# Cross-attention and a routed FFN on one core: score chunks of three banks, one scratch bank, other places for the steps, and a reordered prologue

## The reference, cut to what matters

```python
x = x + xattn(layernorm(x), ctx, ctx, mask, W_q, W_k, W_v, W_o)   # x: 32 x 100 x 128, ctx: 32 x 1444 x 128
x = x + ffn(layernorm(x), gate_w, w1, w2)

def xattn(Q, K, V, ...):          # 16 heads of 8
    q, k, v = Q @ W_q.T, K @ W_k.T, V @ W_v.T
    e = exp(clip(q k^T / sqrt(8), -50, 50))      # 100 x 1444 for each head
    return (e / sum(e)) v @ W_o.T

def ffn(x, ...):                  # 8 experts, hidden 512, the best 2 for each token
    probs = softmax(x @ gate_w); best two, weights normalised
    return sum of weight * (gelu(x @ w1[e]) @ w2[e])
```

## Time and profile before

| | us |
|---|---|
| median of 3 runs | 1036.55 |
| lowest and highest | 1033.01, 1038.11 |
| the profiled execution | 1029.2 |
| its span, first to last instruction | 1027.4 |
| first scores | 29.69 |
| one batch of the loop, mean of eight | 25.68 |

### The profile page before, as it was taken

How to read it: one execution, slowest core, us unless ns; L and a number is a source line. 1 busy time by engine, 2 the same in 40 slices (tenths; PEclk the granted TensorE clock), 3 DMA queues, 4 the chain that set the end, 5 groups by cost and what they waited for, 6 DMA issues and landing times.

```text
span 1027.4 us, 31365 instructions
## 1 busy us (share of the span) xinstructions
PE 953.8 (93%) x9974; PEld 695.5 (68%) x9975; DVE 808.5 (79%) x2140; ACT 716.0 (70%) x941; POOL 340.0 (33%) x422
## 2 busy tenths in 40 slices
PE   3799999999999999999999999999999996599980
PEld 2566666666666666666666666666666773599980
DVE  5477888888888888888888888888888985444433
ACT  2577878787878787878787878787878774244430
POOL 3182322222222222222222222222222234255554
PEclk9699999999999999999999999999999999699995
DMA  6755666666666666666666666666666663122216
GB/s 182 182 150 173 186 189 188 186 188 189 186 188 186 189 187 189 186 189 188 187 186 189 186 189 186 189 186 187 189 188 186 184 229 86 41 66 67 66 43 191
DMA packets 312438, 172.70 MB, mean 168 GB/s; under 512 B 205274, under 2 KB 260518, under 8 KB 312406
## 3 DMA queue, kind: packets, MB, share of 16 engines
q1 hardware_dynamic: 131898, 142.19, 42.4%
q10 hardware_dynamic: 175612, 23.48, 14.5%
q0 software_dynamic: 4896, 6.63, 2.1%
HBM read 36.83 MB, written 22.08 MB: 57 GB/s over the span
## 4 chain that ended last, share of the span: by engine, by line
PE 88%; DMA 2%; ACT 2%; issue 2%; SPq 2%; DVE 1%; POOL 1%; ACTq 1%; POOLq 0%; DVEq 0%
PE scores L816 32%; PE o_sum L828 28%; PE scratch L747 7%; PE scratch L756 7%; PE scores L940 5%; PE scores L951 5%; ACT probs L1058 2%; SPq L604 1%; DMA q_stack<-q_rep 1%; ACTq L979 1%; PE scratch L794 1%; DMA x_all<-in_x_dram 1%; PE scratch L751 0%; DMA q_and_ctx<-expert_outputs 0%; POOL rows L688 0%
## 5 line engine op out<-in xcount | busy, mean ns | idle before, releaser
L1058 ACT ACTIVATE probs<-scores 128x800 f32<-128x800 f32 (+1 forms) x640 | 603.8, 973 | 152.2 <-PE scores L816 139.8
L816 PE MATMUL scores<-q_stack,k_stack 128*128 128x400 f32 x1536 | 412.9, 385 | 15.2 <-DMA q_stack<-q_rep 9.2
L1214 DVE TENSOR_SCALAR probs<-probs 128x800 f32<-128x800 f32 (+1 forms) x640 | 402.4, 661 | 16.9 <-ACT probs L1058 11.8
L816 PEld LDWEIGHTS scores<-q_stack,k_stack 128*128 128x128 f32 x1536 | 250.8, 190 | 140.8 <-ACT probs L1058 84.1
L828 PE MATMUL o_sum<-probs,v_both 128*17 128x200 f32 x6144 | 304.0, 335 | 0.0
L828 PEld LDWEIGHTS o_sum<-probs,v_both 128*17 128x17 f32 x6144 | 158.4, 97 | 109.3 <-issue 39.9
L699 POOL DMA_INDIRECT expert_rows<-rows,row_atu x64 | 71.9, 1124 | 322.0 <-DVE row_atu L1301 290.2
L756 PE MATMUL scratch<-w_turned,ctxT 128*128 128x128 f32 x768 | 101.0, 275 | 0.0
L756 PEld LDWEIGHTS scratch<-w_turned,ctxT 128*128 128x128 f32 x768 | 99.7, 191 | 0.7 <-issue 0.3
L747 PE MATMUL scratch<-ctxT,w_turned 128*128 128x512 f32 x186 | 85.3, 567 | 0.0
L1154 DVE COPY v_both<-scratch 128x512 f32<-128x512 f32 x93 | 63.7, 685 | 20.4 <-PE scratch L756 20.4
(11 more groups left out here) (148 smaller groups left out, 665.7 us busy)
## 6 DMA issues: line engine op xcount, KB each, us to landing
k_stack<-k_hi SPq DMA_DIRECT2D x192, 256.0 KB, 3.5
k_stack<-k_lo SPq DMA_DIRECT2D x192, 256.0 KB, 4.8
expert_rows<-fill SPq DMA_DIRECT2D x32, 406.2 KB
q_and_ctx<-in_ctx_dram ACTq DMA_DIRECT2D x15, 720.0 KB
ctx_nat<-in_ctx_dram ACTq DMA_DIRECT2D x15, 720.0 KB
q_rep<-q_parts SPq DMA_DIRECT2D x126, 50.0 KB
q_stack<-q_rep SPq DMA_DIRECT2D x126, 50.0 KB, 2.6
v_both<-expert_rows SPq DMA_DIRECT2D x57, 65.0 KB, 1.8
```

The source lines that it names most:

```text
L816: last = nc.tensor.matmul(score_banks(c)[:, m, :], k_stack[p][:, g, t * P:(t + 1) * P], q_stack[p][:, :, g, :], start=True, stop=True)
L1058: nc.scalar.activation(probs_of(c), score_banks(c), ACT.Exp, scale=SCALE).then_inc(exp_ready, 1)
L1214: nc.vector.tensor_scalar(chunk, chunk, LOW, HIGH, ALU.max, ALU.min).then_inc(probs_ready, 1)
```

## The change

The prologue: POOL clears the query stacks ahead of the first deviations; TensorE projects the first queries ahead of the first key third; ScalarE issues the last part of x and the context load of batch 2 after the exp of chunk 2 of batch 0, no longer ahead of chunk 0. In the loop ScalarE issues the context load of batch b+3 after the exp of chunk 12 of batch b, no longer that of batch b+2 ahead of chunk 0, and two more batches stand behind its loop. VectorE's third context transpose, no longer the first, waits for the load of the overhanging keys.

Chunks: 16 of three units, in two times three banks. One scratch bank is left, so every step uses the same one. Steps, PV halves, transposes, norms and queries have other iterations, counted in 16 and no longer in 20; the order of the steps is another one, with value 0 first and value 1 ahead of the tokens.

```diff
-    UNITS = [3, 2, 3, 2, 3, 2, 3, 2, 2, 2] * 2
+    UNITS = [3] * 16
+    SCRATCH = 1
-    SB0, SB1 = 3, 2
+    SB0, SB1 = 3, 3
-    HALF_AT = [5] * 3 + [8] * 3 + [9] * 2 + [11] * 2 + [15] * 6 + [21] * 4 + [23] * 4
+    HALF_AT = [4] * 2 + [5] * 2 + [7] * 3 + [10] * 3 + [12] * 4 + [15] * 7 + [17] * 3
-    STEPS = [("key", 0), ("project", 0), ("value", 0), ("key", 1), ("key", 2), ("tokens", 0), ("gate", 0),
-             ("value", 1), ("value", 2), ("rank", 0)]
-    STEP_AT = [7, 9, 12, 14, 14, 15, 16, 17, 19, 19]
+    STEPS = [("value", 0), ("key", 0), ("project", 0), ("key", 1), ("value", 1), ("tokens", 0), ("gate", 0),
+             ("key", 2), ("value", 2), ("rank", 0)]
+    STEP_AT = [2, 4, 5, 7, 8, 10, 11, 12, 13, 15]
-    TURN_AT = [0, 7, 11]
-    WEIGHED = 5
-    SPLIT_AT = 15
+    TURN_AT = [0, 1, 1]
+    WEIGHED = 4
+    SPLIT_AT = 11
+    LOAD_AT = 12
+    LATE_X_AT = 2
-    CONTEXT_AT = [3, 6, 8]
-    NORM_AT = [[5, 9, 15], [1, 4, 8, 11]]
-    QUERY_AT = [[6, 10, 17], [2, 5, 10, 13]]
+    CONTEXT_AT = [1, 5, 9]
+    NORM_AT = [[3, 6, 10], [0, 3, 6, 9]]
+    QUERY_AT = [[5, 8, 12], [2, 5, 8, 11]]
-    MOMENTS_AT = {8: 4, 9: 5, 10: 6, 11: 7}
+    MOMENTS_AT = {6: 4, 7: 5, 8: 6, 9: 7}
...
-            invert_deviations(0)
             for p in range(2):
                 nc.gpsimd.memset(q_stack[p][:].bitcast(F32), 0.0).then_inc(q_stack_cleared, 1)
+            invert_deviations(0)
...
             pe.wait_ge(w_turned_ready, 1)
+            pe.wait_ge(ctxT_ready, 2)
-            first_key(0)
             pe.wait_ge(xT_ready, 1)
             project_q(scores[:, 1, :]).then_inc(q_in_psum, 1)
+            first_key(0)
...
-            act.dma_start(x_all[:, X_PARTS[2], :], x[X_PARTS[2]].rearrange("b q d -> q b d")).then_inc(x_loaded[2], 16)

             def attend(b, p):
-                if not (isinstance(b, int) and b + 2 >= B):
...
-                    load_blocks(b + 2, p)
                 for c in range(CHUNKS):
...
                     nc.scalar.activation(probs_of(c), score_banks(c), ACT.Exp, scale=SCALE).then_inc(exp_ready, 1)
+                    if not later(b) and c == LATE_X_AT:
+                        act.dma_start(x_all[:, X_PARTS[2], :], x[X_PARTS[2]].rearrange("b q d -> q b d")).then_inc(x_loaded[2], 16)
+                        load_blocks(2, 0)
+                    if c == LOAD_AT and not (isinstance(b, int) and b + 3 >= B):
+                        if later(b):
+                            act.wait_ge(ctxT_ready, turns_before(b + 1) + KSTEPS)
+                        else:
+                            act.wait_ge(scratch_filled, scratch_step(0, FIRST_STEPS[0].index(("turn", KSTEPS - 1))) + 1)
+                        load_blocks(b + 3, 1 - p)
...
                 if k == 0:
                     dve.wait_ge(ctx_loaded[1 - p], 16 * (i + 1 + p))
+                if k == KSTEPS - 1:
                     dve.wait_ge(ctx_over_loaded[1 - p], 16 * (OVER * (i + p) + 1))
```

More of the change, by code:

```diff
@@ L142, in xattn_moe @@
     X_PARTS = [slice(0, QB), slice(QB, 4 * QB), slice(4 * QB, B)]
-    MOMENTS_AT = {8: 4, 9: 5, 10: 6, 11: 7}
+    MOMENTS_AT = {6: 4, 7: 5, 8: 6, 9: 7}
     BEFORE = ITS_BASE[1] + len(PLANS[1]) - 2 * len(STEPS)
-    assert len(STEPS) == len(STEP_AT) and len(STEPS) % 2 == 0 and BEFORE >= 0
+    assert len(STEPS) == len(STEP_AT) and len(STEPS) % SCRATCH == 0 and BEFORE >= 0
     assert 1 + len(NORM_AT[0]) + len(NORM_AT[1]) == QSTEPS
@@ L160, in scratch_use @@
         if is_first(b):
-            return (ITS_BASE[b] + n) % 2, (ITS_BASE[b] + n) // 2
+            return (ITS_BASE[b] + n) % SCRATCH, (ITS_BASE[b] + n) // SCRATCH
         use = BEFORE + n
-        return use % 2, len(STEPS) // 2 * b + use // 2
+        return use % SCRATCH, len(STEPS) // SCRATCH * b + use // SCRATCH
     def planned(b, c):
@@ L323, in xattn_moe @@
         o_sum = ps("o_sum", [P, 512])
-        scratch = ps("scratch", [P, 2, 512])
+        scratch = ps("scratch", [P, SCRATCH, 512])
         hidden_in = [scores[:, n, :] for n in range(2)]
@@ L363, in xattn_moe @@
         scratch_filled = sem("scratch_filled")
-        scratch_emptied = [sem(f"scratch_emptied{n}") for n in range(2)]
+        scratch_emptied = [sem(f"scratch_emptied{n}") for n in range(SCRATCH)]
         k_hi_ready = sem("k_hi_ready")
@@ L862, in _ @@
             for step, (name, k) in enumerate(ALONE):
-                into_scratch(name, k, 0, 0, None, (step % 2, step // 2))
+                into_scratch(name, k, 0, 0, None, (step % SCRATCH, step // SCRATCH))
             pe.wait_ge(mask_cast, 1)
@@ L1039, in _ @@
                     nc.scalar.copy(v_ones[0][:, k * KC:(k + 1) * KC, :, 0:2 * DH],
-                                   scratch[:, step % 2, :].rearrange("p (t n d) -> p t n d", t=KC, n=PAIRS)
-                                   ).then_inc(scratch_emptied[step % 2], 1)
+                                   scratch[:, step % SCRATCH, :].rearrange("p (t n d) -> p t n d", t=KC, n=PAIRS)
+                                   ).then_inc(scratch_emptied[step % SCRATCH], 1)
                 if k == 0:
                     first_stack()
-            act.dma_start(x_all[:, X_PARTS[2], :], x[X_PARTS[2]].rearrange("b q d -> q b d")).then_inc(x_loaded[2], 16)
             def attend(b, p):
-                if not (isinstance(b, int) and b + 2 >= B):
[L1048 to L1051, removed]
-                    load_blocks(b + 2, p)
                 for c in range(CHUNKS):
@@ L1065, in _ @@
             attend(1, 1)
-            with act.Fori(1, B // 2 - 1) as i:
+            with act.Fori(1, B // 2 - 2) as i:
                 attend(2 * i, 0)
                 attend(2 * i + 1, 1)
+            attend(B - 4, 0)
+            attend(B - 3, 1)
             attend(B - 2, 0)
```

## The result

| us | before | after |
|---|---|---|
| median of the runs (lowest to highest) | 1037.33 (1033.01 to 1041.27, 4 runs) | 1048.73 (1046.98 to 1053.33, 4 runs) |
| the profiled execution, its span | 1029.2, 1027.4 | 1048.35, 1046.5 |
| first scores | 29.69 | 21.45 |
| batch 2 begins | 93.0 | 98.1 |
| one batch of the loop | 25.70 | 26.20 |

The change made the kernel slower: 1.0118 times the time of before (95% interval 1.0066 to 1.017). The forecast was 1026.7 us, faster, in a range of 1012 to 1045; both failed.

The account below looks back on a forecast made before the run. TensorE was taken as the loop's bound (24.9 us of work in 25.68), the late query stack ahead of it. Prologue -7, clock -3.5, doubled steps +5.5, loop -4.8 gave -9.8: 1036.55 to 1026.7 us, range 1012 to 1045.

Parts of the forecast that it names:

- the tokens: In each loop batch TensorE would wait 0.3 us at the tokens step for POOL's rows, where before it had none.
- the second rival: Longer clips hold POOL, which becomes the bound: batch 26.7 us, kernel 1062, or about 1045 at half of it; chance 0.18.
- Both cost nothing: In the loop, loading context b+3 at chunk 12 and waiting for its overhang at transpose 2 would cost 0 us.
- no stall, at most 2 us: In batch 0, the rest of x, issued after chunk 2's exp, would cause no stall, at most 2 us.
- the boundary without a wait: At the batch boundary, moving the context load to chunk 12 would remove a wait of 0.55 us a batch.
- Doubled steps +5.5: In the first two batches, two steps in one iteration share one bank: 4.9 us, plus 0.6 for neighbouring iterations.
- First scores at 21 to 24 us: Ahead of the loop, a sign that the forecast holds: scores start at 21 to 24 us; after 26 it is wrong.
- the 7 us: Prologue: earlier clearing and later loads of x and context 2 gain 7 of 7.8 us; low bound 2.2.
- Loop -0.16 a batch: The loop batch falls from 25.68 to 25.5 us, 0.16 less; over 30 batches -4.8 us.
- waits of 0.3 and 0.3: Added per loop batch to 24.9 us of TensorE work: 0.3 for scores behind exp, 0.3 at the tokens.
- the first rival: No new wait: POOL's chain ends in time, the loop gains 20 to 24 us, kernel about 1010; chance 0.17.
- The -3.5 us: After the first scores TensorE's clock is not halved, so about 12 us of matmuls run faster: 3.5 of a possible 6.

Follow-up runs that it names:

- e7: The changed kernel with the prologue and context issues of the kernel before; 1046.56 us, 1.0107 times the kernel before.
- e10: e7 with POOL signalling after the first of its two rows, which is all the tokens step reads; 1024.31 us, 0.9895 times the kernel before.
- e11: The changed kernel with VectorE's clips of chunks 4 to 8 cut into two halves; 1060.82 us, 1.0225 times the kernel before.
- e9: e5 with the late part of x issued ahead of chunk 0 and batch 2's context at chunk 3 of batch 0; 1025.45 us, 0.9893.
- e1: The changed kernel with POOL signalling after the first of its two rows; 1055.32 us, 1.0223 times the kernel before.
- e2: The changed kernel with the third keys ahead of tokens and gate in the order of steps; 1041.71 us, 1.0074 times the kernel before.
- e8: e4 with x at chunk 2, batch 2's context at chunk 6 of batch 0, later contexts at a batch's start; 1025.77 us, 0.9904.
- e4: The kernel before with the change's prologue and context issues, its own chunks, banks and step order; 1046.13 us, 1.0133.
- e5: e1 with context issues from batch 3's on back ahead of a batch's first exp; 1024.11 us, 0.9886 times the kernel before.
- e3: The changed kernel with SyncE, not ScalarE, issuing the late part of x and contexts of batches 2 and 3; 1052.34 us, 1.0213.

## Why the prediction was wrong

**The step that failed first: the tokens.** "From the token to the end of the second row of POOL is 524.45 - 518.45 = 6.0" was carried over from before, though the same change makes every clip long and puts other work of VectorE beside the rows. It became 6.5, and the wait 0.5 us and not 0.3; without it the batch falls from 26.19 (e7) to 25.52 (e10), so it cost 0.67 a batch, 20 us. This was the second rival, at half its size: I had put its turning point at 0.33 us more in the chain, and 0.5 came. I had priced the rival at +0.4 for the deviation and +0.8 for the rows. In the batches shown the deviation gave +0.21, the two rows together +0.57, and the power -0.28, which I hadn't counted. Of the rows it is the first that grew, by 0.96, and it is the one with new neighbours, the key subtraction and a clip. So where the rows fall seems to have counted for more than the length of a clip; no run changed that alone. The rule that I cited for the rival (the Trainium skill, SBUF — State Buffer, Who interferes with whom) is borne out by e11, with 625 against 1251 ns. I had it and a row that agreed, and still gave it 0.18 "against" rows that fall elsewhere. Rows that fall elsewhere are indeed short, 812 to 816 ns beside a copy out of scratch; but I didn't look where the new order would put them.

**The step that failed second: the moved issues.** "Both cost nothing", I wrote of the load at chunk 12, and "no stall, at most 2 us" of the pair at chunk 2. I hid the issue at chunk 12 behind an exp of 1.17 us, which only does for the 0.56 us that it took elsewhere, and priced the pair at chunk 2 by the lateness of x. What counts is what is still on the queue. In batches 0 and 1 of the changed kernel this is the gap between 76.6 us and e9's 71 with nothing held: 5.5 us. In its loop it cost nothing only because the tokens' wait made the batch long enough for the queue to empty, or nearly; e1, e2 and e11 took the wait away, left the issue in its place, and paid 32, 20 and 38 us of held issues.

**What held.** Norms of about 1.15 us (1.11) and the boundary without a wait: so. Doubled steps +5.5: batches 0 and 1 take 70 (e10) and 71 us (e9), against 63.3 before and 64.5 in e8, so 6.5 to 7. First scores at 21 to 24 us: 21.45, but the sum gave the 7 us to the moved prologue alone. The moves suffice with two banks (e8, 21.05), and without them the one bank gets to 23.65 (e10), which I hadn't counted; so in this kernel the moves brought 2.2 us against e10 and 4.4 against e7, and that the forecast was met is in part luck. Loop -0.16 a batch: 25.70 to 25.52 once the tokens don't wait, -0.18. That is luck too: my waits of 0.3 and 0.3 were to stand on 24.9 us of work, with the 0.25 of shorter waits for exp dropped without a reason, and in e10 the tokens don't wait. No run came near 24.9, the loop of the first rival; whether TensorE's work is more than I added up, or waits for clips and exp remain behind its modelled ends, is open.

**The clock.** The -3.5 us assumed 1.00 after the first scores. It was 0.50 from 30 to 36 us, with a hold ahead of it here and without one in e9, and low again from 56 to 60 (0.58), behind the second hold; in the kernel before it was 0.50 from 30 to 42. So some low clock was saved, and not all of it. What either stretch cost wasn't measured apart.

**The sum.** The prologue alone is worth 0.9904 (e8), the scores without the wait 0.9895 (e10), some 10 us each: both halves were worth taking. Each was undone by one thing of its own: e4 against e8 by where contexts are issued, +20 us; e7 against e10 by which row is waited for, +22. Together they give no more than one: 1024.11 (e5) and 1025.45 (e9). For e9 the places are known: e10, without the moved prologue, starts its scores at 23.65 and e9 at 21.44, and both then need 70 to 71 us for batches 0 and 1, so there was little left to add. These are the best found, some 1% below the kernel before and not told apart by their intervals. Two banks in the first two batches might give both gains; that wasn't tried.

**Open.** The kernel before ran between 1029.2 and 1047.0 us on the chips of this study, and its profiled execution is at the low end; that is why spans differ by 19 us and medians by 11. What changes from run to run in it was not looked into. One candidate: the profiled executions of e5, e8 and e10 each have one loop batch that is some 3 to 6 us longer than its like, in which VectorE waits 3.5 to 4.7 us for a late context. e2's batch of 25.83 without a wait that I could name is open too.

## What to carry to other kernels

An issue costs what is left on its queue: before a transfer is moved, look when the one ahead of it on the same queue ends, what else moves at that time, and not at what the issue took at its old place. A stall may be what gives a queue time to empty; whoever removes one must see what ran in its shadow, and judge by the batch, since here two true repairs (e1, e11) would have been dropped by their totals. A price on one engine depends on what another does beside it: when an order changes, look at what the new neighbours will be. And a consumer should wait for the part that it reads: a semaphore on the first row was worth 2% (e7 to e10).

## What the runs showed of the hardware

- A context issue kept its whole engine from new work when many packets of an earlier transfer were left on that queue: over six runs never with up to 110 left, always with over 300, for 0.9 to 5.2 us in the loop. It ended with 95 to 308 still left. On SyncE four issues behind a context took 18.46 us (e3).
- A context of 720 KB in 5764 packets took 20 to 23 us from its first packet to its last in the kernel before, and up to 28.6 in e1: 387 packets a us on average when the queue had the engines (e1, 156 to 162 us), 24 while SyncE's key transfers had 97% of their time (167 to 172).
- VectorE's clip of 1200 columns doubled a POOL instruction on 100 numbers, 1251 against 625 ns beside halves of it (e11), and that instruction ended 35 to 38 ns behind a clip in four kernels.
- TensorE's granted clock went from 1.00 to 0.50, the 1.2 GHz level, behind four of e1's ten held issues, which had made TensorE wait; behind two others as long it stayed at 1.00.
